# Adaptive layer norm block, 32 sequences: the second norm moved from VectorE to ScalarE, the pooling sum to GpSimd

## The chip, the cores and the metric

The kernel runs on one core of a Trainium2 chip. A core has TensorE (PE in the profile; its weight loads are PEld), VectorE (DVE), ScalarE (ACT), GpSimd (POOL) and the sync engine (SP), which here only issues DMAs. The metric is the device time of one execution in microseconds; smaller is better.

## The reference, cut to what matters

There are 32 sequences (B) of 256 positions (S) of 128 numbers (D). Each goes through a layer norm, an attention block with a local window and a pooled "latent" branch, a gated residual addition, a second layer norm and a small network with weights mixed from eight experts.

```
h = layernorm(x) * (1 + ca) + sa
GK = pool(h @ wgk)                # mean over 4 neighbouring positions: 64 latents
x = x + ga * attention(h)         # local windows of 32, and the 64 latents
h = layernorm(x) * (1 + cb) + sb  # the second norm
x = x + gb * experts(h)           # layernorm(x) = (x - mean) / sqrt(var + 1e-5)
```

## The kernel before, in words

Each engine has its own program, written out by hand; semaphores order them. An engine carries its instructions out in the order in which they stand, and one that waits holds back all that stands behind it.

The first part is a software pipeline over the 32 sequences (`pipeline`, L201). Passage `it` works on up to five sequences, each at another stage: first norm and hT for sequence it (lag 0), projections, scores and maxima for it - 1 (lag 1), exponentials, transposes, values and denominators for it - 2 (lag 2), output projection and residual for it - 3 (lag 3), second norm, h2T and the hidden sum of the gate for it - 4 (lag 4). Passages 0 to 3 are written out, 4 to 31 are a loop, 32 to 35 are written out again. The second part, from about 598 us, applies the mixed expert weights in four groups of eight sequences, and the change does not touch it.

What stands in which order in one passage, as far as the prediction speaks of it:

- VectorE: the maxima and subtractions of the scores (L561, L568), the statistics of both norms (`stats`, L543, giving mv_a and mv_d), then both normalisations (`normed`, L553 to L556, called in L608 for xn_a and in L615 for xn_d), the reciprocal and products of the latent branch (L620 to L629), y_ga (L591), then the reciprocal rden of the local denominators (L639) when TensorE has given them, a_loc (L641), the pooling sum hpT over four positions (L645), the gated products a_gated and rem_g (L652, L654) and the latent maxima (L576), and then the scores of the next sequence.
- GpSimd: the masked keys KM (L347), for each norm ve = var + eps and rstd = ve ** -0.5 (`inv_std`, L335 to L340, on two columns of 128), the two halves of PT_sum (L360), GKBD (L366), the residual addition (L372) and attT (L379).
- ScalarE: copies and exponentials (L413 to L431), then the copies of PL (L438, L441), the four copies of PT out of PSUM (L448), h2T (L452), the ReLU with its sum (L456), hT (L464), the exponentials of the latent branch (L470), tanh (L475).
- TensorE: projections (L851 to L871), the transposes of the latent and local probabilities (L909 to L915, L901), the latent values (L951), which wait for both PL copies, the output projection (L992), the transposes of xn_d (L999), which wait for xn_d, then the values (L932), which wait for all four PT copies, and the denominators (L936), which wait for both halves of PT_sum and release rden. Then r_out (L1006), the gate's first layer (L1016), the transposes of xn_a (L1023), the latent scores (L975) and the scores (L888).

At the start GpSimd also issues DMAs: the scale rows ga to DRAM and, after they have landed, broadcast back as GA (L387, L389), and the expert weights TW (L330, L332). SP issues all other loads, those of the keys KBD (L277) among them, for which the first scores wait.

Of the kernel before, what the change touches and what calls it, by code (L numbers as in the profile page):

```python
# [23 lines left out]
def adaln_block(nc, ins, out):  # L24
# [18 lines left out]
    with ExitStack() as ctx:  # L43
        def sb(name, shape, dt=F32):
            return ctx.enter_context(nc.sbuf_tensor(name, shape, dt))

        def sem(name):
            return ctx.enter_context(nc.semaphore(name))
# [59 lines left out]
        mv_a, mv_d = sb("mv_a", [P, T, 2]), sb("mv_d", [P, T, 2])  # L108
        ve_a, ve_d = sb("ve_a", [P, T]), sb("ve_d", [P, T])
        rstd_a, rstd_d = sb("rstd_a", [P, T]), sb("rstd_d", [P, T])  # L110
        xn_a, xn_d = sb("xn_a", [P, T, D]), sb("xn_d", [P, T, D])
        hT, hpT = sb("hT", [P, S]), sb("hpT", [P, NL])


        QT = [sb(f"QT{k}", [P, S]) for k in range(2)]
# [39 lines left out]
             "ga_ready", "ga_stored", "ga_loaded", "wqT_done", "wqT_ready", "attn_w_ready", "gate_w_done",  # L155
             "gate_w_ready", "masks_ready", "wT_done", "wT_ready"))
        (stat_a, aggr_a, eps_a, rstd_a_s, xn_a_s, xT_done, hT_ready, hp_ready, qk_done, qt_ready, km_ready,
         k_ready, kbd_loaded, pts_ready, gqk_done, gq_ready, gkbd_ready) = (sem(n) for n in (
             "stat_a", "aggr_a", "eps_a", "rstd_a_s", "xn_a_s", "xT_done", "hT_ready", "hp_ready", "qk_done",
             "qt_ready", "km_ready", "k_ready", "kbd_loaded", "pts_ready", "gqk_done", "gq_ready", "gkbd_ready"))  # L160
        (s_ready, mx_ready, s_sub, p_ready, gv_done, gvbd_ready, v_done, vrows_ready, v_stored, vbd_loaded,
         masks_loaded, ls_ready, lmx_ready,
         ls_sub, pl_ready, gates_done, tg_ready) = (sem(n) for n in (
# [149 lines left out]
        def _(pool):  # L313
# [4 lines left out]
                                    pattern=[[-1, P]], channel_multiplier=1).then_inc(mask_ready, 1)  # L318
            nc.gpsimd.memset(minus_half[:], -0.5).then_inc(mask_ready, 1)
            nc.gpsimd.memset(eps_row[:], 1e-5).then_inc(mask_ready, 1)  # L320
            nc.gpsimd.memset(r_out[:], 0.0).then_inc(zeros_ready, 1)
            nc.gpsimd.memset(tri[:], 1.0).then_inc(mask_ready, 1)
            nc.gpsimd.memset(KBD[:], 0.0).then_inc(zeros_ready, 1)
            pool.wait_ge(mask_ready, 5)
            nc.gpsimd.affine_select(out=tri[:], in_=tri[:], compare_op=ALU.is_ge, fill=0.0, base=0,
                                    pattern=[[-1, P]], channel_multiplier=1).then_inc(mask_ready, 1)
            nc.gpsimd.memset(VBD[:], 0.0).then_inc(pv_done, 1)
# [14 lines left out]
            def step(it):  # L342
                if has(it, 1):

                    b = it - 1
                    pool.wait_ge(k_ready, b + 1)
                    nc.gpsimd.tensor_tensor(KM[:], bc(K_ch[:], [P, 4, S], 1), bc(bd_scale[:], [P, 4, S], 2), ALU.mult  # L347
                                            ).then_inc(km_ready, 1)
                if has(it, 0):
                    inv_std(it, aggr_a, mv_a, ve_a, eps_a, rstd_a, rstd_a_s)  # L350
                if has(it, 4):
                    inv_std(it - 4, aggr_d, mv_d, ve_d, eps_d, rstd_d, rstd_d_s)
                if has(it, 2):

                    b = it - 2
                    both = PT[:, 0:G * 2 * S].rearrange("p (g k s) -> p g k s", g=G, k=2)
                    for t in range(T):
                        pool.wait_ge(pt_copied, 4 * b + 2 * (t + 1))
                        tile = slice(t * P, (t + 1) * P)
                        nc.gpsimd.tensor_tensor(PT_sum[:, :, tile], both[:, :, 0, tile], both[:, :, 1, tile], ALU.add  # L360
                                                ).then_inc(pts_ready, 1)
                if has(it, 1):

                    b = it - 1
                    pool.wait_ge(gq_ready, 2 * (b + 1))
                    nc.gpsimd.tensor_tensor(GKBD[0:NL], bc(GKT[:], [NL, LH, NL], 1),  # L366
                                            bc(head[0:NL, 0:LH], [NL, LH, NL], 2), ALU.mult).then_inc(gkbd_ready, 1)
                if has(it, 3):
                    b = it - 3
                    pool.wait_ge(yga_ready, b + 1)  # L370
                    xb = x_all[:, bass.ds(b * S, S)]
                    nc.gpsimd.tensor_tensor(xb, xb, y_ga[:], ALU.add).then_inc(x1_ready, 1)  # L372
                if has(it, 2):
                    b = it - 2

                    pool.wait_ge(ag_ready, b + 1)
                    pool.wait_ge(remg_ready, b + 1)
                    at_least(pool, y_done, b)
                    nc.gpsimd.tensor_tensor(attT[:], a_gated[:], rem_g[:], ALU.add).then_inc(att_ready, 1)  # L379

            def after(it):
                if it == 0:
# [14 lines left out]
        def _(act):  # L397
# [9 lines left out]
            def step(it):  # L407
# [21 lines left out]
                    nc.scalar.copy(V_rows[:].rearrange("p t n -> p (t n)"), WB[3][:, 0:T * D]).then_inc(vrows_ready, 1)  # L429
                if has(it, 2):  # L430
                    probs(it - 2, 3)  # L431
                if has(it, 2):
                    b = it - 2
                    if isinstance(it, int) and it == 2:
                        act.wait_ge(ga_stored, 16)

                    act.wait_ge(lpt_done, 2 * b + 1)
                    nc.scalar.copy(PL[:, :, 0:S].rearrange("p g (t s) -> p t g s", t=T),  # L438
                                   WB[0][:].rearrange("p (t g s) -> p t g s", t=T, g=LG)).then_inc(lpt_copied, 1)
                    act.wait_ge(lpt_done, 2 * b + 2)  # L440
                    nc.scalar.copy(PL[:, :, S:S + P],  # L441
                                   WB[1][:, 0:2 * P].rearrange("p (g s) -> p g s", g=LG)).then_inc(lpt_copied, 1)
                    for q in range(4):

                        act.wait_ge(pt_done, 4 * b + (q + 1))
                        t, gp = divmod(q, 2)
                        dst = PT[:, gp * 4 * S:(gp + 1) * 4 * S].rearrange("p (k s) -> p k s", s=S)[:, :, t * P:(t + 1) * P]
                        nc.scalar.copy(dst, SB[q][:].rearrange("p (k s) -> p k s", s=P)).then_inc(pt_copied, 1)  # L448
# [62 lines left out]
        def _(dve):  # L511
# [83 lines left out]
            def step(it):  # L595
# [9 lines left out]
                if has(it, 0):  # L605
# [2 lines left out]
                    normed(x_all[:, bass.ds(it * S, S)], mv_a, rstd_a, xn_a, xn_a_s)  # L608
                    if isinstance(it, int) and it == 0:
                        modulation()  # L610
                if has(it, 4):
                    b = it - 4
                    dve.wait_ge(rstd_d_s, b + 1)
                    at_least(dve, x2T_done, b)
                    normed(x_all[:, bass.ds(b * S, S)], mv_d, rstd_d, xn_d, xn_d_s)  # L615
                if has(it, 2):

                    b = it - 2
# [16 lines left out]
                if has(it, 2):  # L635
# [3 lines left out]
                    nc.vector.reciprocal(rden[:], SB[2][:, S:2 * S]).then_inc(rden_ready, 1)  # L639
                    dve.wait_ge(rden_ready, b + 1)  # L640
                    nc.vector.tensor_tensor(a_loc[:], SB[2][:, 0:S], rden[:], ALU.mult).then_inc(a_ready, 1)  # L641
                if has(it, 0):

                    dve.wait_ge(hT_ready, it + 1)
                    nc.vector.tensor_reduce(hpT[:], hT[:].rearrange("p (n k) -> p n k", k=POOL), AX.X, ALU.add  # L645
                                            ).then_inc(hp_ready, 1)
                if has(it, 2):
                    b = it - 2
                    dve.wait_ge(a_ready, b + 1)
# [52 lines left out]
            def after(it):  # L702
# [6 lines left out]
                if it == 0:  # L709
# [12 lines left out]
                        then(nc.vector.tensor_scalar(size[:], size[:], 0.25, None, ALU.max))  # L722
                        then(nc.vector.scalar_tensor_tensor(dst[:], sign[:], -1.0, size[:], ALU.add, ALU.mult))
                    nc.vector.memset(wait_carrier[:], 0.0).then_inc(ga_ready, 1)
                    dve.wait_ge(mask_ready, 6)
                    then(nc.vector.tensor_copy(ones_bd[:].rearrange("p (h d) -> p h d", h=4), bc(quad[:], [P, 4, HD], 2)))
                    then(nc.vector.tensor_scalar(pool_bd[:], ones_bd[:], 1.0 / POOL, None, ALU.mult))

# [414 lines left out]
```

## Time and profile before

| what | us |
|---|---|
| median of 2 runs | 773.5 (773.03 and 773.96) |
| span of the profiled execution | 772.4 |
| one passage of the loop, rden to rden | 16.26 |
| PE busy | 701.8 |
| DVE busy | 582.3 |
| ACT busy | 371.3 |
| POOL busy | 292.9 |

The profile is one execution. Its span runs from the first to the last instruction; the median stands 1.1 us above it, and I take that for what lies around the span in the profiled execution too, whose own time is then about 773.5. In a timeline row the first number is the start in us from the span's start, the second the time from the first start to the last end of the merged instructions. Busy shares are averages; what bounds the kernel is read from the chain of waits and from the timelines of one passage.

### The profile page before, as it was taken

The numbers are of one execution on the slowest core, as the hardware profiler recorded it, in microseconds if no ns is written. First come the engines' busy times: TensorE is split into PE (matmuls) and PEld (weight loads), VectorE is DVE, ScalarE is ACT, GpSimd is POOL, SyncE is SP. The second block draws the span as 40 slices with busy tenths as digits, with TensorE's granted clock in tenths as the row PEclk, the third lists the DMA queues.
The fourth block names the chain that finished last, engine by engine and source line by source line (L and its number), as shares of the span: only waits on it lengthen the run. The fifth ranks groups of instructions, "written<-read, shape, count | busy, mean of one in ns | idle before, by whom it ended". The sixth has DMA issues, their size and how long they took to land.

```text
span 772.4 us, 21515 instructions
## 1 busy us (share of the span) xinstructions
PE 701.8 (91%) x7542; PEld 505.3 (65%) x7542; DVE 582.3 (75%) x1313; ACT 371.3 (48%) x878; POOL 292.9 (38%) x351
## 2 busy tenths in 40 slices
PE   5239989999999999999999999999977999999998
PEld 3016656655666656666566666566647989898996
DVE  5326879999989999999999899998885537264542
ACT  2015646555665556655566655566541342433133
POOL 4205635544556445555445564455541000000000
PEclk9569999999999999999999999999996999999999
DMA  3764933222222222232222322222250010000101
GB/s 89 206 73 77 122 57 78 52 60 48 48 65 64 54 54 48 54 75 51 58 48 48 72 57 55 54 48 53 65 62 1 1 35 20 27 27 14 28 20 48
DMA packets 85316, 42.79 MB, mean 55 GB/s; under 512 B 40552, under 2 KB 83880, under 8 KB 85168
## 3 DMA queue, kind: packets, MB, share of 16 engines
q1 hardware_dynamic: 83840, 36.21, 20.7%
q0 software_dynamic: 1456, 6.31, 5.2%
q8 instruction: 13, 0.21, 0.1%
q14 instruction: 7, 0.06, 0.0%
HBM read 16.13 MB, written 8.40 MB: 32 GB/s over the span
## 4 chain that ended last, share of the span: by engine, by line
PE 52%; DVE 22%; issue 10%; POOL 8%; DMA 3%; ACT 2%; SPq 1%; DVEq 1%; POOLq 0%; ACTq 0%
DVE mx L561 10%; PE SB L888 8%; PE SB L836 7%; PE WB L824 7%; DVE xn_d L555 5%; PE WB L975 5%; PE SB L932 4%; PE WB L811 4%; PE SB L811 4%; POOL rstd_d L340 2%; PE WB L1006 2%; POOL rstd_a L340 2%; DMA KBD<-KM 2%; PE SB L936 2%; PE SB L1016 2%
## 5 line engine op out<-in xcount | busy, mean ns | idle before, releaser
L888 PE MATMUL SB<-KBD,QT 128*32 128x512 f32 x1024 | 118.2, 603 | 22.6 <-DMA KBD<-KM 21.6
L347 POOL TENSOR_TENSOR KM<-K_ch,bd_scale 128x1024 f32<-128x1024 f32 x32 | 60.6, 1894 | 142.9 <-ACT K_ch L413 142.9
L561 DVE TENSOR_REDUCE mx<-SB 128x8 f32<-128x512 f32 x128 | 86.7, 678 | 22.9 <-PE SB L888 22.9
L888 PEld LDWEIGHTS SB<-KBD,QT 128*32 128x32 f32 x1024 | 30.6, 111 | 106.3 <-issue 106.3
L506 ACT ACTIVATE Pr<-WB,mb1T 128x256 f32<-128x256 f32 x128 | 49.9, 478 | 75.3 <-PE WB L824 75.3
L360 POOL TENSOR_TENSOR PT_sum<-PT 128x512 f32<-128x512 f32 x64 | 82.1, 1302 | 10.3 <-ACT PT L448 10.3
L568 DVE TENSOR_TENSOR Pr<-SB,mx 128x512 f32<-128x512 f32 x128 | 84.1, 677 | 0.0
L405 ACT ACTIVATE Pr<-Pr 128x512 f32<-128x512 f32 x128 | 80.9, 632 | 5.0 <-DVE Pr L568 1.7
L639 DVE RECIPROCAL rden<-SB 128x256 f32<-128x256 f32 x32 | 56.2, 1757 | 18.9 <-PE SB L936 18.9
L448 ACT COPY PT<-SB 128x512 f32<-128x512 f32 x128 | 65.1, 597 | 0.0
L901 PE MATMUL SB<-ident,Pr 128*128 128x128 f32 x512 | 61.8, 273 | 1.4 <-ACT Pr L405 1.4
L836 PE MATMUL SB<-Pr,GA 128*128 128x256 f32 x256 | 61.0, 381 | 0.0
L824 PE MATMUL WB<-h2T,KBD 128*128 (+1 forms) x256 | 60.2, 380 | 0.0
L901 PEld LDWEIGHTS SB<-ident,Pr 128*128 128x128 f32 x512 | 56.8, 141 | 2.3 <-ACT Pr L405 2.3
L379 POOL TENSOR_TENSOR attT<-a_gated,rem_g 128x256 f32<-128x256 f32 x32 | 23.5, 733 | 89.9 <-DVE a_gated L652 86.8
L555 DVE TENSOR_SCALAR xn_d<-x_all,mv_d,rstd_d 128x128 f32 (+1 forms) x64 | 45.4, 751 | 13.5 <-POOL rstd_d L340 13.5
L824 PEld LDWEIGHTS WB<-h2T,KBD 128*128 128x128 f32 x256 | 48.2, 190 | 6.4
L470 ACT ACTIVATE PlA<-PlA 128x256 f32<-128x256 f32 x32 | 13.3, 417 | 79.4 <-DVE PlA L582 79.4
L836 PEld LDWEIGHTS SB<-Pr,GA 128*128 128x128 f32 x256 | 46.1, 190 | 5.9 <-DVE GA L680 1.0
L975 PE MATMUL WB<-GKBD,GQT 128*128 128x512 f32 (+1 forms) x128 | 47.9, 498 | 0.0
L456 ACT ACTIVATE SB<-SB,gate_b 128x256 f32<-128x256 f32 x32 | 14.3, 448 | 67.3 <-PE SB L1016 67.3
L470 ACT ACTIVATE PlB<-PlB 128x512 f32<-128x512 f32 x32 | 20.1, 630 | 47.5 <-DVE PlB L582 47.5
(190 smaller groups left out, 1484.0 us busy)
## 6 DMA issues: line engine op xcount, KB each, us to landing
KBD<-KM SPq DMA_DIRECT2D x128, 128.0 KB, 2.4
x_all<-in_L_attn_x SPq DMA_DIRECT2D x32, 128.0 KB, 2.1
v_rows<-V_rows SPq DMA_DIRECT2D x32, 128.0 KB, 1.8
TW<-in_L_ffn_TW POOLq DMA_DIRECT2D x16, 256.0 KB, 8.7
VBD<-v_rows SPq DMA_DIRECT2D x128, 32.0 KB, 1.9
GA<-ga_rows POOLq DMA_DIRECT2D x1, 2048.0 KB, 9.9
out_x<-attT SPq DMA_DIRECT2D x16, 128.0 KB, 1.8
out_x<-y_ga SPq DMA_DIRECT2D x16, 128.0 KB, 1.8
```

The source lines that it names most:

```text
L360: nc.gpsimd.tensor_tensor(PT_sum[:, :, tile], both[:, :, 0, tile], both[:, :, 1, tile], ALU.add).then_inc(pts_ready, 1)
L405: nc.scalar.activation(Pr[:, k, :], Pr[:, k, :], ACT.Exp).then_inc(p_ready, 1)
L448: nc.scalar.copy(dst, SB[q][:].rearrange("p (k s) -> p k s", s=P)).then_inc(pt_copied, 1)
L555: nc.vector.tensor_scalar(xn[:, t, :], src[:, t * D:(t + 1) * D], mv[:, t, 0:1], rstd[:, t:t + 1], ALU.subtract, ALU.mult).then_inc(xn_s, 1)
L561: nc.vector.tensor_reduce(mx[:, k, :], SB[k][:].rearrange("p (h j) -> p h j", h=8), AX.X, ALU.max).then_inc(mx_ready, 1)
L568: nc.vector.tensor_tensor(Pr[:, k, :].rearrange("p (w h c) -> p h w c", w=2, h=8), SB[k][:].rearrange("p (h w c) -> p h w c", w=2, h=8), b ...
L811: last = mm((WB if m < 8 else SB)[m % 4][:, k * P:(k + 1) * P], lhsT, Gd[:, bass.ds(g * (J * GB), J * GB)], start=True, stop=True)
L824: last = mm(WB[2 * (j % 2) + c // 2][:, (c % 2) * S:(c % 2 + 1) * S], mW1[:, j, c * P:(c + 1) * P], h2T[:, bass.ds((g * GB + j) * S, S)], ...
L836: last = mm(SB[j % 2][:, 0:S], mW2[:, c, j, :], u[j % 2][:, c, :], start=(c == 0), stop=(c == FC - 1))
L888: last = mm(SB[k][W * q:W * q + W, :].rearrange("p (h j) -> p h j", h=8), QT[hh][:, W * blk:W * blk + W], KBD[:, 8 * hh:8 * hh + 8, W * bl ...
L901: last = nc.tensor.transpose(SB[q][:, k * P:(k + 1) * P], Pr[:, q, o:o + P], ident[:])
L975: mm(WB[1 - t][:, 0:8 * m].rearrange("p (h j) -> p h j", h=8), GQT[:, t * P:(t + 1) * P], GKBD[:, :, 0:m], start=True, stop=True).then_inc ...
```

## The change

The pooling sum over four positions leaves VectorE. GpSimd does it as two additions, 256 to 128 columns and 128 to 64, at the end of its passage, where it waits for hT. The normalisation of the second norm leaves VectorE too. GpSimd computes after rstd_d the negated mean (neg_d) and, after waiting for it, shift_d = -mean * rstd; ScalarE computes xn_d as Identity(x * rstd_d + shift_d), two activations of 128x128, before its PL copies. A buffer of -1 is set up at the start.

```diff
+            nc.gpsimd.memset(minus_one[:], -1.0).then_inc(mask_ready, 1)
...
                 if has(it, 4):
+                    at_least(pool, xn_d_s, T * (it - 4))
                     inv_std(it - 4, aggr_d, mv_d, ve_d, eps_d, rstd_d, rstd_d_s)
+                    nc.gpsimd.tensor_tensor(neg_d[:], mv_d[:, :, 0], minus_one[:], ALU.mult).then_inc(neg_d_s, 1)
+                    pool.wait_ge(rstd_d_s, it - 4 + 1)
+                    pool.wait_ge(neg_d_s, it - 4 + 1)
+                    nc.gpsimd.tensor_tensor(shift_d[:], neg_d[:], rstd_d[:], ALU.mult).then_inc(shift_d_s, 1)
...
+                if has(it, 0):
+
+                    pool.wait_ge(hT_ready, it + 1)
+                    nc.gpsimd.tensor_tensor(hp2[:], hT[:].rearrange("p (m k) -> p m k", k=2)[:, :, 0],
+                                            hT[:].rearrange("p (m k) -> p m k", k=2)[:, :, 1], ALU.add).then_inc(hp2_s, 1)
+                    pool.wait_ge(hp2_s, it + 1)
+                    nc.gpsimd.tensor_tensor(hpT[:], hp2[:].rearrange("p (n k) -> p n k", k=2)[:, :, 0],
+                                            hp2[:].rearrange("p (n k) -> p n k", k=2)[:, :, 1], ALU.add).then_inc(hp_ready, 1)
...
                 if has(it, 2):
                     probs(it - 2, 3)
+                if has(it, 4):
+                    b = it - 4
+                    act.wait_ge(shift_d_s, b + 1)
+                    at_least(act, x2T_done, b)
+                    for t in range(T):
+                        nc.scalar.activation(xn_d[:, t, :], x_all[:, bass.ds(b * S + t * D, D)], ACT.Identity,
+                                             scale=rstd_d[:, t:t + 1], bias=shift_d[:, t:t + 1]).then_inc(xn_d_s, 1)
...
-                if has(it, 4):
-                    b = it - 4
-                    dve.wait_ge(rstd_d_s, b + 1)
-                    at_least(dve, x2T_done, b)
-                    normed(x_all[:, bass.ds(b * S, S)], mv_d, rstd_d, xn_d, xn_d_s)
...
-                if has(it, 0):
-
-                    dve.wait_ge(hT_ready, it + 1)
-                    nc.vector.tensor_reduce(hpT[:], hT[:].rearrange("p (n k) -> p n k", k=POOL), AX.X, ALU.add
-                                            ).then_inc(hp_ready, 1)
```

The order on ScalarE in the loop, from the last exponential to h2T, before. ISA and REGISTER_ALU rows compute addresses and semaphore values; they are no work on data.

```order
L405 ACTIVATE Pr<-Pr 128x512 [waits s_sub]
L437 ISA
L438 COPY PL<-WB 128x2x2x128 [waits lpt_done]
L440 REGISTER_ALU
L441 COPY PL<-WB 128x2x128 [waits lpt_done]
L445 REGISTER_ALU
L448 COPY PT<-SB 128x4x128 [waits pt_done] x4
L451 REGISTER_ALU
L452 ISA [waits x2T_done]
```

And in the changed kernel:

```order
L420 ACTIVATE Pr<-Pr 128x512 [waits s_sub]
L449 REGISTER_ALU
L190 REGISTER_ALU [waits shift_d_s]
L452 ISA [waits x2T_done]
L452 ACTIVATE xn_d<-x_all,shift_d,rstd_d 128x128
L452 ISA
L452 ACTIVATE xn_d<-x_all,shift_d,rstd_d 128x128
L459 ISA
L460 COPY PL<-WB 128x2x2x128 [waits lpt_done]
L462 REGISTER_ALU
L463 COPY PL<-WB 128x2x128 [waits lpt_done]
L467 REGISTER_ALU
```

The two activations that write xn_d, and the wait for shift_d ahead of them, now stand ahead of the PL and PT copies, which stand unchanged behind them.

The order on GpSimd in the loop, from rstd_a to PT_sum, before:

```order
L340 TENSOR_TENSOR rstd_a<-ve_a,minus_half 128x2 [waits eps_a]
L337 ISA
L338 TENSOR_TENSOR ve_d<-mv_d,eps_row 128x2 [waits aggr_d]
L340 TENSOR_TENSOR rstd_d<-ve_d,minus_half 128x2 [waits eps_d]
L358 ISA
L360 TENSOR_TENSOR PT_sum<-PT 128x4x128 [waits pt_copied]
L358 REGISTER_ALU
L360 TENSOR_TENSOR PT_sum<-PT 128x4x128 [waits pt_copied]
```

And in the changed kernel, where the last row's wait, pt_copied, is for ScalarE's PT copies:

```order
L342 TENSOR_TENSOR rstd_a<-ve_a,minus_half 128x2 [waits eps_a]
L190 ISA
L339 ISA [waits xn_d_s]
L340 TENSOR_TENSOR ve_d<-mv_d,eps_row 128x2 [waits aggr_d]
L342 TENSOR_TENSOR rstd_d<-ve_d,minus_half 128x2 [waits eps_d]
L356 TENSOR_TENSOR neg_d<-mv_d,minus_one 128x2
L359 TENSOR_TENSOR shift_d<-neg_d,rstd_d 128x2 [waits neg_d_s,rstd_d_s]
L365 ISA
L367 TENSOR_TENSOR PT_sum<-PT 128x4x128 [waits pt_copied]
```

Two more instructions, neg_d and shift_d, stand between rstd_d and PT_sum.

The order on GpSimd at the start, from the first norm of passage 1 to the broadcast of GA, before:

```order
L338 TENSOR_TENSOR ve_a<-mv_a,eps_row 128x2 [waits aggr_a]
L340 TENSOR_TENSOR rstd_a<-ve_a,minus_half 128x2 [waits eps_a]
L366 TENSOR_TENSOR GKBD<-GKT,head 64x512 [waits gq_ready]
L387 DMA ga_rows<-PT 32x128 [waits ga_ready]
L389 DMA GA<-ga_rows 128x4096 [waits ga_stored]
```

And in the changed kernel, where hp is the buffer hp2:

```order
L340 TENSOR_TENSOR ve_a<-mv_a,eps_row 128x2 [waits aggr_a]
L342 TENSOR_TENSOR rstd_a<-ve_a,minus_half 128x2 [waits eps_a]
L373 TENSOR_TENSOR GKBD<-GKT,head 64x512 [waits gq_ready]
L390 TENSOR_TENSOR hp<-hT 128x128 [waits hT_ready]
L393 TENSOR_TENSOR hpT<-hp 128x64 [waits hp2_s]
L402 DMA ga_rows<-PT 32x128 [waits ga_ready]
L404 DMA GA<-ga_rows 128x4096 [waits ga_stored]
```

The two additions, which wait for hT of passage 1, now stand ahead of the DMAs of ga, GA and the expert weights.

## Rows read from the trace of the kernel before

**Rows 1.** The page, the chain that ended last, shares by engine.

```profile
PE 52%; DVE 22%; issue 10%; POOL 8%; DMA 3%; ACT 2%; SPq 1%; DVEq 1%; POOLq 0%; ACTq 0%
```

**Rows 2.** The chain of waits around 345 us: start, us, what.

```profile
345.36 1.30 DVE xn_d L555
...
346.71 0.44 PE SB L999 x2
```

**Rows 3.** Timeline of VectorE, one passage: start, us, instruction, [idle before].

```profile
332.52 1.76 DVE L639 RECIPROCAL rden<-SB 128x256 f32<-128x256 f32 x1 [0.34 <-PE SB L936]
...
334.67 0.42 DVE L645 TENSOR_REDUCE hpT<-hT 128x64 f32<-128x256 f32 x1
335.01 0.42 DVE L652 SCALAR_TENSOR_TENSOR a_gated<-tg,a_loc 128x256 f32<-128x256 f32 x1
...
344.16 0.60 DVE L555 TENSOR_SCALAR xn_a<-x_all,mv_a,rstd_a 128x128 f32 x2 [0.34 <-POOL rstd_a L340]
345.10 1.55 DVE L555 TENSOR_SCALAR xn_d<-x_all,mv_d,rstd_d 128x128 f32 x2 [0.33 <-POOL rstd_d L340]
...
348.78 1.76 DVE L639 RECIPROCAL rden<-SB 128x256 f32<-128x256 f32 x1 [0.32 <-PE SB L936]
```

**Rows 4.** Timeline of ScalarE, the same passage.

```profile
343.36 0.57 ACT L438 COPY PL<-WB 128x512 f32<-128x512 f32 x1
343.82 0.37 ACT L441 COPY PL<-WB 128x256 f32<-128x256 f32 x1
...
347.41 0.57 ACT L452 ACTIVATE h2T<-SB,sbT,cb1T 128x256 f32 x1 [1.29 <-PE SB L999]
```

**Rows 5.** Timeline of GpSimd, the same passage.

```profile
344.09 0.20 POOL L338 TENSOR_TENSOR ve_d<-mv_d,eps_row 128x2 f32<-128x2 f32 x1
344.37 0.69 POOL L340 TENSOR_TENSOR rstd_d<-ve_d,minus_half 128x2 f32<-128x2 f32 x1
```

**Rows 6.** Timeline of TensorE, the same passage.

```profile
342.47 1.91 PE L901 MATMUL SB<-ident,Pr 128*128 128x128 f32 x16
344.31 0.42 PE L951 MATMUL WB<-PL,GVBD 128*32 128x128 f32 x8
...
348.64 0.71 PE L1006 MATMUL WB<-rem_n,r_out 128*128 128x128 f32 x4
```

**Rows 7.** Timeline of all engines, first passage after the loop.

```profile
555.07 0.57 ACT L438 COPY PL<-WB 128x512 f32<-128x512 f32 x1
...
556.95 2.53 POOL L360 TENSOR_TENSOR PT_sum<-PT 128x512 f32<-128x512 f32 x2 [1.11 <-ACT PT L448]
...
559.53 0.64 PE L936 MATMUL SB<-PT_sum,ones_bd 128*32 128x256 f32 x8 [0.34 <-POOL PT_sum L360]
...
560.24 1.76 DVE L639 RECIPROCAL rden<-SB 128x256 f32<-128x256 f32 x1 [1.28 <-PE SB L936]
...
562.49 0.42 DVE L652 SCALAR_TENSOR_TENSOR a_gated<-tg,a_loc 128x256 f32<-128x256 f32 x1
```

**Rows 8.** ScalarE groups by form: line, op, shapes, count | busy us, mean ns | idle.

```profile
L452 ACT ACTIVATE h2T<-SB,sbT,cb1T 128x256 f32 x28 | 15.9, 567 | 35.3 <-PE SB L999 35.3
...
L429 ACT COPY V_rows<-WB 128x256 f32<-128x256 f32 x32 | 11.4, 357 | 0.7 <-PE WB L863 0.7
...
L494 ACT COPY gate_w1T<-WB 128x128 f32<-128x128 f32 x1 | 0.3, 266 | 0.6 <-PE WB L1083 0.6
```

**Rows 9.** Timeline of TensorE, the loop's first passage.

```profile
101.71 1.44 PE L932 MATMUL SB<-PT,VBD 128*32 128x64 f32 x48 [2.84 <-issue]
...
103.99 1.08 PE L1006 MATMUL WB<-rem_n,r_out 128*128 128x128 f32 x4
```

**Rows 10.** Busy time by stretch: us, PE, PEld, DVE, ACT, POOL, PEclk, DMA, GB/s.

```profile
101.00:105.00 4.00, 3.29 (x62) 2.48 (x63) 0.90 (x1) 0.00 (x0) 0.44 (x1) 0.57 0.11 23
```

**Rows 11.** Timeline of the start, GpSimd and TensorE.

```profile
24.74 0.72 POOL L387 DMA_DIRECT2D ga_rows<-PT  x1
...
50.00 5.39 PE L888 MATMUL SB<-KBD,QT 128*32 128x512 f32 x32 [21.57 <-DMA KBD<-KM]
```

More of the change, by code:

```diff
@@ L110, in adaln_block @@
         rstd_a, rstd_d = sb("rstd_a", [P, T]), sb("rstd_d", [P, T])
+        minus_one, neg_d, shift_d = sb("minus_one", [P, T]), sb("neg_d", [P, T]), sb("shift_d", [P, T])
         xn_a, xn_d = sb("xn_a", [P, T, D]), sb("xn_d", [P, T, D])
-        hT, hpT = sb("hT", [P, S]), sb("hpT", [P, NL])
+        hT, hp2, hpT = sb("hT", [P, S]), sb("hp2", [P, S // 2]), sb("hpT", [P, NL])
         QT = [sb(f"QT{k}", [P, S]) for k in range(2)]
@@ L157, in adaln_block @@
         (stat_a, aggr_a, eps_a, rstd_a_s, xn_a_s, xT_done, hT_ready, hp_ready, qk_done, qt_ready, km_ready,
-         k_ready, kbd_loaded, pts_ready, gqk_done, gq_ready, gkbd_ready) = (sem(n) for n in (
+         k_ready, neg_d_s, shift_d_s, hp2_s, kbd_loaded, pts_ready, gqk_done, gq_ready, gkbd_ready) = (sem(n) for n in (
              "stat_a", "aggr_a", "eps_a", "rstd_a_s", "xn_a_s", "xT_done", "hT_ready", "hp_ready", "qk_done",
-             "qt_ready", "km_ready", "k_ready", "kbd_loaded", "pts_ready", "gqk_done", "gq_ready", "gkbd_ready"))
+             "qt_ready", "km_ready", "k_ready", "neg_d_s", "shift_d_s", "hp2_s", "kbd_loaded", "pts_ready", "gqk_done", "gq_ready", "gkbd_ready"))
         (s_ready, mx_ready, s_sub, p_ready, gv_done, gvbd_ready, v_done, vrows_ready, v_stored, vbd_loaded,
@@ L323, in _ @@
             nc.gpsimd.memset(KBD[:], 0.0).then_inc(zeros_ready, 1)
-            pool.wait_ge(mask_ready, 5)
+            pool.wait_ge(mask_ready, 6)
             nc.gpsimd.affine_select(out=tri[:], in_=tri[:], compare_op=ALU.is_ge, fill=0.0, base=0,
@@ L724, in after @@
                     nc.vector.memset(wait_carrier[:], 0.0).then_inc(ga_ready, 1)
-                    dve.wait_ge(mask_ready, 6)
+                    dve.wait_ge(mask_ready, 7)
                     then(nc.vector.tensor_copy(ones_bd[:].rearrange("p (h d) -> p h d", h=4), bc(quad[:], [P, 4, HD], 2)))
```

## The prediction

> **What bounds the kernel now.** I read the shares of the chain first, then the chain around one passage of the loop, then the timelines of the engines in that passage, at last the passages that have no partner in the loop.
>
> The chain lies on TensorE for 52%, on VectorE for 22% and on GpSimd for 8% [rows 1]: no single engine sets the end, a ring through several does. In the passage from 332.52 to 348.78 it runs from VectorE to rstd_d on GpSimd (344.37 for 0.69) [rows 5], from there to xn_d on VectorE, and from there to TensorE's transposes at 346.71 [rows 2]. Behind these stand the values and denominators, which release rden, and with rden VectorE begins anew: rden to rden is 348.78 - 332.52 = 16.26 us [rows 3]. So xn_d is on the path. Its two instructions take 1.55 us where the same two for xn_a take 0.60 [rows 3], since the second runs into GpSimd's PT_sum.
>
> There is a second way through the passage, and it decides here. ScalarE starts the PL copies at 343.36 [rows 4], 1.7 us before rstd_d is ready (344.37 + 0.69 = 345.06) [rows 5], and the PT copies follow them, then PT_sum, the denominators, rden. In passage 32, which has no first norm, this way is what arrives last: PL copy 555.07, PT_sum 556.95, denominators 559.53 after a wait of 0.34 us for PT_sum, rden 560.24 [rows 7]. From PL to rden it is 5.17 us; in the loop 348.78 - 343.36 = 5.42 [rows 3, 4]. So the second way is only 0.25 us shorter than the one through xn_d. Whatever delays the PL copies by more than 0.25 us delays the passage.
>
> **The change part by part.**
>
> **The pooling sum** leaves VectorE. The row is 0.42 us, but without it a_gated begins 562.49 - 560.24 = 2.25 us after rden instead of 335.01 - 332.52 = 2.49 [rows 3, 7]: a gain of 0.24 us, because the wait for a_loc is then bare. VectorE works without a break from rden to the statistics, so all of it counts, and rstd_d ends at 345.06 - 0.24 = 344.82. On GpSimd the two additions stand behind attT. TensorE reads hpT only in its next projections, behind all the scores, and GpSimd waits for ScalarE meanwhile, so I put them at nothing (bounds 0 and +1 a passage, if the stride of two made them several times slower).
>
> **neg_d and shift_d.** Two operations on two columns. The nearest row is ve_d, 0.20 us, with the next starting 0.28 after it; the other is rstd_d, a power, 0.69 [rows 5]. I take the first, a product being nearer to a sum: neg_d starts at the end of rstd_d less some 0.04 of overlap, shift_d 0.28 later, and ends 0.20 after that, at 344.82 - 0.04 + 0.28 + 0.20 = 345.26. Bound from above: 0.69 each, +1.0. Behind them waits PT_sum, but that will be later anyway.
>
> **xn_d on ScalarE.** ScalarE's order puts it ahead of PL. This is the heart of it: PL and PT need nothing from the second norm and now wait for it. ScalarE's start behind a wait with an address computed after it: the transposes end at 346.71 + 0.44 = 347.15, h2T starts at 347.41, so 0.26 [rows 2, 4]; VectorE needed 0.04 (345.06 to 345.10) [rows 3, 5], which is the lower bound. I take 0.27: start 345.53. One Identity with scale and bias from columns takes 0.567 for 256 columns; copies of 256 and 128 columns differ by 0.357 - 0.266 = 0.091 [rows 8], so 0.476 each. Each starts 0.11 before the one ahead of it ends, as the two PL copies do (343.36 + 0.57 against 343.82) [rows 4], and an address stands between them, 0.05: together 0.476 + 0.476 - 0.11 + 0.05 = 0.89. Bounds: 0.27 + 0.17, as for plain copies, and 0.567 whole, twice. The PL copy may start 0.11 before their end, at 345.53 + 0.89 - 0.11 = 346.31. That is 2.95 us later than 343.36. Then the 5.17 of the second way: rden at 351.48, a passage of 351.48 - 332.52 = 18.96, which is 2.7 us more than 16.26. The bounds taken together give +2.0 and +3.9.
>
> The xn_d that VectorE loses gives nothing back: its 1.55 us were worth 0.25, up to where the second way takes over, and that way is now 3 us late.
>
> **TensorE.** Its transposes of probabilities end at 342.47 + 1.91 = 344.38, or 344.14 with the gain above; the latent values start 0.95 us after the PL copy (343.36, 344.31) [rows 4, 6], so at 347.26. Today there is no gap there; the changed kernel has one of 3.1 us in each passage. What such a gap does, one place shows: in the loop's first passage TensorE stood idle 2.84 us before 101.71 [rows 9], and in 101 to 105 its mean granted clock was 0.57, so it had fallen from 2.4 to 1.2 GHz and came back [rows 10]. The work lost is (1 - 0.57) x 4 = 1.7 us; 0.34 of it would lie in TensorE's wait for PT_sum [rows 7], so a fall costs at most 1.4 on the path. The r_out group took 1.08 instead of 0.71 us [rows 6, 9], which says that part of it lies behind rden, where TensorE is ahead. I take 1.0 (bounds 0 and 1.4), and 8 passages in 10, because one gap with one fall doesn't say that each has it.
>
> The Trainium skill (TensorE: Matmul & The Clock Gate, HAM oscillation) describes a kernel whose TensorE waits in each tile, is set back to half clock each time and pays each time. By that rule every passage falls: 27 x 1.4 = 38 us instead of the 21 that I enter. The row of the loop's first passage agrees with the rule, for one gap.
>
> **Outside the loop.** 27 passages of the loop are alike (4 to 31 without the first). The first has the idle 2.84 us already, and I let ScalarE's wait fall into it: 0 (bounds -2 and +3). In passages 32 and 33, where the statistics come earlier, the same reckoning gives +1.9 and +2.5, and in 34 and 35 the longer way to xn_d +0.3: 4.7.
>
> **The start.** The first scores wait 21.57 us for the keys, which land at 50.00, while GA and the expert weights are being moved [rows 11]. The changed kernel has the two additions ahead of those DMAs: the one at 24.74 starts 1 to 2 us later, while VectorE, which no longer waits for hT, makes the masks about 1 us sooner. So the keys get ahead of part of the other traffic. I take -4 (bounds -15, where it all falls away, and +1).
>
> **The sum.** 27 x 2.7 = 73; + 0 + 4.7 - 4 = 74; the clock 27 x 0.8 x 1.0 = 21; in all +95. The profiled execution's own time is its span 772.4 and about 1.1 around it, 773.5, which is the median of the runs shown. 773.5 + 95 = 868.5; I say 868.
>
> **The rivals.**
>
> Clock stays up: the gap of 3.1 us is followed by dense work and TensorE keeps its 2.4 GHz. For it: in the loop's other passages there is hardly an idle time, so the trace has one case only. Against it: that case. 773.5 + 74 = 847.
>
> Faster: ScalarE's wait is harmless, because shift_d would come before the PL copies, and what counts is that the collision of xn_d with PT_sum is gone. The place is the PL copy at 343.36; it decides from the moment when shift_d is ready before it, and it comes at 345.26 by the sum. If it held, the loop would run at the second way's 16.26 - 0.25 - 0.24 = 15.8, 27 x 0.49 = 13 less, and with the start -4: 756. For it: 1.55 against 0.60 us on the path [rows 3]; against it: 1.9 us that cannot go.
>
> The start gives back much more: keys and GA no longer meet, -15 instead of -4: 857. For it: the DMA order; against it: the expert weights follow on the same queues at once.
>
> GpSimd as the bound: the strided additions take several us and TensorE waits for hpT. The price is +1 or more a passage, 895. GpSimd is idle for most of that time, so I give it little.
>
> **How the numbers follow.** Forecast 0.68, clock up 0.17, large gain at the start 0.08, slow additions 0.04, faster 0.02, and 0.01 that the change comes out within 2%, which is about what a measurement of this kernel can tell from no change. Range: from 840 (clock up, and the cheap end of ScalarE's start) to 888 (a fall in each passage at 1.4, which is 885, and a little for GpSimd). Faster 0.02, same 0.01, slower 0.97.
>
> **What would show it.** Right: a passage of 19 to 20.5 us; ScalarE idle about 2 us before xn_d, released by GpSimd's shift_d; the PL copy 3 us later within the passage; TensorE idle some 3 us before the latent values, released by ScalarE, and a granted clock of 0.5 in many short stretches; rden waiting for the denominators and these for PT_sum; the keys landing a few us before 50. Wrong: a passage below 17, PL copies that don't move, a granted clock of 1.00 through the loop (then 847), or TensorE waiting for GpSimd's hpT.

## The result: 858.2 us, 11% slower, and where the time went

The changed kernel takes 858.2 us (median of 2 runs, 856.89 and 859.43) against 773.5, a ratio of 1.108 with a 95% interval from 1.106 to 1.111. Forecast were 868 us and a range from 840 to 888. The profiled execution took 856.89 us, its span is 855.2: 82.8 more than the 772.4 of before.

The page's busy times and the shares of the chain by engine, for the changed kernel (the chain answers to [rows 1]):

```profile
PE 722.6 (85%) x7542; PEld 528.4 (62%) x7542; DVE 530.2 (62%) x1217; ACT 401.2 (47%) x942; POOL 323.4 (38%) x480
...
PE 37%; DVE 27%; issue 17%; POOL 8%; ACT 5%; DMA 2%; DVEq 1%; SPq 1%; ACTq 0%; POOLq 0%
```

VectorE lost 52 us of work (582.3 to 530.2) and the kernel became 85 us longer. ScalarE, which was hardly on the chain, has 5% of it now, and "issue", time in which the profile shows nothing that is waited for, grew from 10% to 17%. TensorE has the same 7542 matmuls and is busy 21 us longer: a sign that it ran part of them at a lower clock.

One passage without a fall of the clock, from rden at 368.96 to rden at 387.93, 18.97 us. GpSimd in it (answers to [rows 5]; start, us, instruction):

```profile
380.59 0.69 POOL L342 TENSOR_TENSOR rstd_d<-ve_d,minus_half 128x2 f32<-128x2 f32 x1
381.24 0.19 POOL L356 TENSOR_TENSOR neg_d<-mv_d,minus_one 128x2 f32<-128x2 f32 x1
381.58 0.20 POOL L359 TENSOR_TENSOR shift_d<-neg_d,rstd_d 128x2 f32<-128x2 f32 x1
384.65 2.52 POOL L367 TENSOR_TENSOR PT_sum<-PT 128x512 f32<-128x512 f32 x2 [2.87 <-ACT PT L470]
```

ScalarE in the same passage (answers to [rows 4]):

```profile
381.98 0.88 ACT L452 ACTIVATE xn_d<-x_all,shift_d,rstd_d 128x128 f32 x2 [2.27 <-POOL shift_d L359]
382.76 0.56 ACT L460 COPY PL<-WB 128x512 f32<-128x512 f32 x1
383.23 0.37 ACT L463 COPY PL<-WB 128x256 f32<-128x256 f32 x1
383.49 2.05 ACT L470 COPY PT<-SB 128x512 f32<-128x512 f32 x4
```

TensorE (answers to [rows 6], and its L948 to the denominators of [rows 7]):

```profile
383.64 0.42 PE L963 MATMUL WB<-PL,GVBD 128*32 128x128 f32 x8 [2.95 <-ACT PL L463]
...
385.31 0.38 PE L1011 MATMUL SB<-ident,xn_d 128*128 128x128 f32 x2
385.67 1.21 PE L944 MATMUL SB<-PT,VBD 128*32 128x64 f32 x64
387.22 0.64 PE L948 MATMUL SB<-PT_sum,ones_bd 128*32 128x256 f32 x8 [0.34 <-POOL PT_sum L367]
387.79 0.71 PE L1018 MATMUL WB<-rem_n,r_out 128*128 128x128 f32 x4
```

VectorE at its end (answers to [rows 3]):

```profile
387.93 1.76 DVE L656 RECIPROCAL rden<-SB 128x256 f32<-128x256 f32 x1 [1.25 <-PE SB L948]
```

Read from top to bottom this is one ring: ScalarE, done with its exponentials, stands idle for 2.27 us until GpSimd has shift_d; then come xn_d, the PL copies, the PT copies, the two halves of PT_sum, the denominators, rden. The latent values on TensorE wait 2.95 us, for PL copies that before were made while the statistics were still being worked out. The transposes of xn_d, for which the second norm is needed at all, don't wait any more.

The waits between 120 and 600 us, in total, times, longest, show that it is so in every passage, once each:

```profile
PE WB L963 <- ACT PL L463: 73.4, 25, 3.0
...
POOL PT_sum L367 <- ACT PT L470: 69.0, 24, 2.9
...
ACT xn_d L452 <- POOL shift_d L359: 56.4, 25, 2.3
```

The next passage, from 387.93 to 407.83, has the same work and takes 19.90. Busy time by stretch (us; PE, PEld, DVE, ACT, POOL with counts; granted clock; share and GB/s of DMA): first the passage without a fall, then this one nearly whole, then four stretches inside it.

```profile
368.96:387.93 18.97, 15.69 (x201) 10.39 (x202) 13.30 (x33) 10.67 (x25) 8.76 (x14) 1.00 0.23 48
387.93:407.80 19.87, 16.94 (x201) 11.56 (x201) 13.31 (x32) 10.68 (x25) 10.48 (x16) 0.91 0.22 46
...
399.50:402.50 3.00, 0.18 (x2) 0.00 (x0) 0.45 (x2) 1.56 (x5) 1.04 (x3) 1.00 0.86 176
402.50:404.00 1.50, 1.39 (x30) 1.25 (x32) 0.00 (x0) 1.50 (x5) 0.39 (x1) 0.51 0.04 8
404.00:406.00 2.00, 2.00 (x24) 1.83 (x20) 1.28 (x3) 0.51 (x2) 2.00 (x2) 0.52 0.00 0
406.00:407.83 1.83, 1.83 (x75) 1.30 (x74) 0.50 (x3) 0.56 (x1) 1.79 (x3) 1.00 0.00 0
```

TensorE is all but idle from 399.5 to 402.5 (0.18 us of work), then is granted 1.2 GHz instead of 2.4 for about 3.5 us, and has its full clock back before rden. Its rows there:

```profile
402.61 0.66 PE L963 MATMUL WB<-PL,GVBD 128*32 128x128 f32 x8 [2.93 <-ACT PL L463]
...
404.66 1.22 PE L1004 MATMUL WB<-w_out_half,attT 128*128 128x128 f32 x4
...
407.14 0.62 PE L948 MATMUL SB<-PT_sum,ones_bd 128*32 128x256 f32 x8
407.69 0.71 PE L1018 MATMUL WB<-rem_n,r_out 128*128 128x128 f32 x4
```

From the latent values to the denominators it takes 407.14 - 402.61 = 4.53 us, against 387.22 - 383.64 = 3.58 without a fall. The 0.34 us of waiting for PT_sum are gone, so the work grew by 1.29 and the path by 0.95; over the whole passage it is 0.93. Of the loop's 27 like passages 20 have such a fall, three in a row and then one without, and on the mean a fall costs 0.87.

The balance of the two spans, from the starts of rden in either trace:

| stretch | before | after | difference |
|---|---|---|---|
| to the first rden | 68.11 | 58.39 | -9.7 |
| the next two passages, the loop's first among them | 35.99 | 35.47 | -0.5 |
| 27 like passages of the loop | 440.11 | 529.57 | +89.5 |
| passages 32 and 33 | 31.43 | 36.74 | +5.3 |
| behind the last rden of the local branch | 196.8 | 195.0 | -1.7 |
| sum | | | +82.8 |

(Differences are taken before rounding.) The +89.5 are 27 times 2.67 for the ring (18.97 against a mean of 16.30) and 20 times 0.87 for the clock: 72.1 and 17.4.

The -9.7 at the start. The issue of the keys' DMAs, of GA's, and the first scores, in the changed kernel ([rows 11] are those of before):

```profile
28.07 2.54 SPq L278 DMA_DIRECT2D KBD<-KM  x4
...
30.12 0.59 POOL L404 DMA_DIRECT2D GA<-ga_rows  x1 [3.17 <-DMA ga_rows<-PT]
...
40.02 5.65 PE L900 MATMUL SB<-KBD,QT 128*32 128x512 f32 x32 [12.74 <-DMA KBD<-KM]
```

In the kernel before, the same two issues stood almost together:

```profile
29.78 2.69 SPq L277 DMA_DIRECT2D KBD<-KM  x4
...
29.97 0.59 POOL L389 DMA_DIRECT2D GA<-ga_rows  x1 [4.50 <-DMA ga_rows<-PT]
```

A lead of the keys of 0.19 us has become one of 2.05, and the scores start 10 us sooner. Experiments 5, 6 and 8 below are about this.

### The profile page after: what moved, and what is told of

The parts are those of the page before. It is cut to its first block, busy times and chain, and to the rows that moved or that the text cites. A ratio compares the mean times of both kernels' runs of the same rounds, so it can differ in the third digit from the quotient of the medians.

```text
span 855.2 us, 21704 instructions
## 1 busy us (share of the span) xinstructions
PE 722.6 (85%) x7542; PEld 528.4 (62%) x7542; DVE 530.2 (62%) x1217; ACT 401.2 (47%) x942; POOL 323.4 (38%) x480
## 4 chain that ended last, share of the span: by engine, by line
PE 37%; DVE 27%; issue 17%; POOL 8%; ACT 5%; DMA 2%; DVEq 1%; SPq 1%; ACTq 0%; POOLq 0%
DVE mx L583 9%; PE SB L848 7%; PE WB L836 7%; DVE rden L656 6%; PE SB L944 4%; PE WB L963 4%; PE WB L823 4%; PE SB L823 3%; PE WB L1004 3%; POOL PT_sum L367 3%; POOL rstd_d L342 3%; PE SB L948 2%; ACT xn_d L452 2%; DVE a_loc L658 2%; DVE st_a L568 2%
## 5 line engine op out<-in xcount | busy, mean ns | idle before, releaser
L900 PE MATMUL SB<-KBD,QT 128*32 128x512 f32 x1024 | 118.5, 604 | 14.4 <-DMA KBD<-KM 12.7
L367 POOL TENSOR_TENSOR PT_sum<-PT 128x512 f32<-128x512 f32 x64 | 80.2, 1274 | 88.9 <-ACT PT L470 88.9
L637 DVE RECIPROCAL rlden<-WB 128x128 f32<-128x128 f32 x32 | 30.6, 958 | 126.4 <-PE WB L963 126.4
L963 PE MATMUL WB<-PL,GVBD 128*32 128x128 f32 x384 | 23.9, 312 | 86.2 <-ACT PL L463 86.2
L583 DVE TENSOR_REDUCE mx<-SB 128x8 f32<-128x512 f32 x128 | 86.7, 677 | 14.7 <-PE SB L900 14.7
L963 PEld LDWEIGHTS WB<-PL,GVBD 128*32 128x32 f32 x384 | 13.4, 118 | 93.6 <-ACT PL L463 93.4
L452 ACT ACTIVATE xn_d<-x_all,shift_d,rstd_d 128x128 f32 (+1 forms) x64 | 28.1, 485 | 72.3 <-POOL shift_d L359 72.3
```

Of the source, the lines that this page charges most:

```text
L583: nc.vector.tensor_reduce(mx[:, k, :], SB[k][:].rearrange("p (h j) -> p h j", h=8), AX.X, ALU.max).then_inc(mx_ready, 1)
L900: last = mm(SB[k][W * q:W * q + W, :].rearrange("p (h j) -> p h j", h=8), QT[hh][:, W * blk:W * blk + W], KBD[:, 8 * hh:8 * hh + 8, W * bl ...
L963: last = mm(WB[0][q:q + W, den * P:(den + 1) * P], ones_bd[:] if den else GVBD[:, k, g, :], PL[:, g, (t + k) * P:(t + k + 1) * P], start=( ...
```

## The experiments

My theory: ScalarE's wait for shift_d, placed ahead of the PL copies, sets the passage, and falls of TensorE's clock in the gap add to it; the pooling sum gains a little by itself. Its rivals: the activations themselves or GpSimd's added work are what costs, wherever they stand; and the lower clock has another cause than the gap. For the start, the theory is that the gain is the keys' lead over GA's transfer; the rival, that it comes from the masks being made sooner.

**1. The normalisation alone.** The changed kernel with the pooling sum back on VectorE:

```diff
-                    pool.wait_ge(hT_ready, it + 1)
...
                     nc.vector.tensor_tensor(a_loc[:], SB[2][:, 0:S], rden[:], ALU.mult).then_inc(a_ready, 1)
+                if has(it, 0):
+
+                    dve.wait_ge(hT_ready, it + 1)
+                    nc.vector.tensor_reduce(hpT[:], hT[:].rearrange("p (n k) -> p n k", k=POOL), AX.X, ALU.add
+                                            ).then_inc(hp_ready, 1)
```

> The second norm's move alone: GpSimd computes shift_d, ScalarE computes xn_d ahead of the PL copies; the pooling sum stays on VectorE. My theory (the whole slowdown comes from ScalarE waiting for shift_d ahead of the PL and PT copies, and from the clock falls behind it): a passage without a fall 18.97 + 0.24 = 19.2 us, falls in about three of four passages, and the keys land at 50 again instead of 40, so about 858 + 6.5 + 10 = 875. Rival (GpSimd's two additions for the pooling are a part of the slowdown): faster than the changed kernel, below 858.

Measured: 876.8 us, ratio 1.133 (1.131 to 1.135). A passage without a fall takes 19.22 us, 0.25 more than with both parts; the gap on TensorE is 3.05 us and about five passages in six have a fall. So the normalisation is the whole loss and more, and the pooling sum is worth 0.25 a passage here too.

**2. The pooling sum alone.** The kernel before with the two additions on GpSimd in place of VectorE's sum.

> The pooling sum's move alone: two additions on GpSimd; the second norm stays on VectorE. My theory: VectorE's stretch is 0.24 us shorter in each passage, 16.30 becomes 16.05, and the keys land about 10 us earlier at the start, so 773.5 - 6.6 - 10 = 757. Rival (TensorE waits for GpSimd's hpT, or the additions delay GpSimd's other work): a passage above 16.3 and 773 or more.

Measured: 757.2 us, ratio 0.979 (0.977 to 0.980). The 27 passages take 433.4 us, 6.7 fewer than before, and the first scores start at 41.02 instead of 50.00. At the first rden 8.0 us of the start's gain are there (60.16 against 68.11); with the passages' 6.7 that is 14.7 of the 16.0 measured, and the rest lies in passages 32 and 33 (0.3) and behind them. The two halves of the change add up nearly: +103.6 and -16.0 make +87.7, measured are +84.7.

**3. The same activations, behind the PT copies.** The changed kernel; the block of xn_d on ScalarE is moved, not altered.

```diff
                 if has(it, 2):
                     probs(it - 2, 3)
-                if has(it, 4):
-                    b = it - 4
-                    act.wait_ge(shift_d_s, b + 1)
...
+                if has(it, 4):
+                    b = it - 4
+                    act.wait_ge(shift_d_s, b + 1)
...
                 if has(it, 4):
                     b = it - 4
                     act.wait_ge(x2T_done, b + 1)
```

> The changed kernel with ScalarE's xn_d block moved behind the four PT copies, ahead of h2T; all else as in the changed kernel. My theory (the place in ScalarE's order is the cause, not the work): the PL copies start 0.24 us earlier in the passage than before, xn_d ends at about the same moment as it did on VectorE, a passage of about 16.4 us, no clock falls in the loop, and with the start's gain of 10 about 766. Rival (the work itself, GpSimd's two more operations and ScalarE's slower xn_d, is the cause): a passage above 18, 815 or more.

Measured: 764.6 us, ratio 0.990 (0.987 to 0.993): 94 us fewer than the changed kernel, by the place of two instructions. ScalarE and TensorE in one passage:

```profile
300.98 0.57 ACT L453 COPY PL<-WB 128x512 f32<-128x512 f32 x1
...
301.71 2.04 ACT L463 COPY PT<-SB 128x512 f32<-128x512 f32 x4
303.61 0.90 ACT L469 ACTIVATE xn_d<-x_all,shift_d,rstd_d 128x128 f32 x2
...
304.57 0.44 PE L1011 MATMUL SB<-ident,xn_d 128*128 128x128 f32 x2 [0.73 <-ACT xn_d L469]
```

The activations take 0.90 us as before and have no idle time ahead of them; the passage is 16.32 us and the 27 like passages have no fall. So neither the activations nor GpSimd's work are the cost; the wait in front of PL is. It also shows that the move gains nothing even here: 16.32 against 16.03 with xn_d on VectorE (experiment 2), because xn_d is now ready only after the PT copies, at 304.51, and TensorE waits 0.73 us for it.

**4 and 9. Filling the gap on TensorE.** The changed kernel; in the gap TensorE makes ten (then eighteen) transposes of the identity into a free half of a PSUM bank, which nobody reads. The ring stays as it is.

```diff
+                if has(it, 4):
+                    for k in range(10):
+                        nc.tensor.transpose(WB[3][:, 2 * P + (k % 2) * P:3 * P + (k % 2) * P], ident[:], ident[:])
                 pe.wait_ge(lpt_copied, 2 * (b + 1))
```

> The changed kernel with ten transposes of the identity on TensorE, into columns of WB3 that nothing reads then, ahead of the wait for the PL copies, so that its idle time of 2.95 us in a passage becomes some 0.6. The waits stay. If the falls of the granted clock make three of four passages 0.8 to 0.9 us longer, they go: all passages 18.97 us, granted clock 1.00 through the loop, 858 - 18 = 840. Rival (the longer passages have another cause and the falls are only seen beside them): still 19.8 in three of four and 858; or the ten transposes themselves delay the latent values, then above 858.

> As e4_fill with 18 transposes instead of ten: e4's ten took 1.26 us and left 1.85 us of idle time in a passage, behind which the clock still fell in 6 of 27 passages; 18 take 2.3 and leave 0.8. Clock theory: no fall left in the loop, all 27 passages 18.97, granted clock 1.00 there, about 843.5 - 6 = 838. Rival (some falls have another cause than the idle time): falls stay, 843.

Measured: 843.5 us with ten (ratio 1.091, 1.089 to 1.093) and 840.6 with eighteen (1.086, 1.084 to 1.089). Ten of them take only 1.26 us where I had expected about 2.3, so that 1.85 us of the gap stayed; eighteen leave 0.97. The stretches of the loop, first the changed kernel, then ten, then eighteen (the last one only up to 600 us; over all its 27 like passages, 512.03 us, the clock is 1.00 too); columns as above, the granted clock is the third number from the end:

```profile
93.86:623.43 529.57, 447.91 (x5401) 303.41 (x5402) 359.24 (x865) 288.28 (x675) 258.37 (x379) 0.94 0.22 47
```

```profile
93.30:610.14 516.84, 460.35 (x5671) 315.21 (x5672) 359.22 (x864) 288.07 (x675) 259.31 (x380) 0.98 0.22 48
```

```profile
93.30:600.00 506.70, 472.84 (x5796) 330.44 (x5788) 357.71 (x860) 283.86 (x666) 255.71 (x376) 1.00 0.22 48
```

Passages with a fall: 20, 6 and none of 27. TensorE does more work in each of these and the kernel gets shorter, by 17.6 us from the changed kernel to the one with eighteen; the 27 passages alone give 17.5 (529.57 against 512.03), which is the 17.4 of the balance. With the clock up all passages take 18.96: the ring by itself. So the lower clock comes from the gap.

The falls over all runs, by the idle time ahead of the latent values: 3.05 us, five in six (experiment 1); 2.95, 20 of 27; 1.85, 6 of 27; 0.97, none. The Trainium skill (TensorE: Matmul & The Clock Gate, HAM oscillation) has TensorE set back in each tile of a kernel that waits some 3 to 5 us for a DMA in each. The gap here is a little shorter, 2.95 us, and the clock fell in three passages of four, and in fewer with a shorter gap; that every passage falls, as the prediction worked out from that rule, did not come.

**5 and 6. The start: GA's DMAs held back.** The kernel before; GpSimd waits ahead of the ga, GA and TW DMAs, for the second hT (experiment 5) or until the first keys have landed (6).

```diff
                     pool.wait_ge(ga_ready, 1)
+                    pool.wait_ge(hT_ready, 2)
```

In experiment 6 the added line is another:

```diff
+                    pool.wait_ge(kbd_loaded, 64)
```

> The kernel before, but GpSimd waits for hT of passage 1 ahead of the DMAs of ga, GA and the expert weights (the place where the changed kernel's additions hold them back); VectorE's masks are not earlier. Theory A (the start's gain of 10 us comes from the weights' DMAs standing later): keys at about 40 us, 764. Theory B (it comes from the masks and with them the keys' own DMAs being issued 1.7 us sooner, and GA's DMA, which waits for the landing of ga, moves by only 0.2): keys within 2 us of 50, 773.

> The kernel before, but GpSimd issues the DMAs of ga, GA and the expert weights only when the first keys have landed. Both theories of the start: with no GA and expert traffic beside them the four key DMAs of 128 KB need a few us each and the keys are there at about 34 instead of 50, unless TensorE then waits for the values' blocks or for GA: between 757 and 765. If the keys' time is set by something else than that traffic (the masks' own packets): still about 48 and 772.

Measured: 766.2 us (ratio 0.990, 0.988 to 0.992) and 763.3 (0.987, 0.985 to 0.989). The scores start at 43.25 and at 34.10. In experiment 5 GA's issue moved by 1.33 us (29.97 to 31.30), and the keys' not at all; that alone is worth 6.75 us at the scores. In experiment 6 much of the 15.9 us is gone again soon: at the first rden 10.9 are left (57.24 against 68.11), mostly since TensorE stands still for 4.02 us in the middle of the values of that passage, on nothing that the profile names ("issue"), and the next three passages take 1.5 us more together than before. Whether GA's later transfer is behind either was not looked into.

**8. The start: the additions behind the DMAs.** Experiment 2, but in passage 1 GpSimd issues its DMAs first and adds afterwards, so that only VectorE's half of the effect is left.

```diff
-                if has(it, 0):
+                if has(it, 0) and not (isinstance(it, int) and it == 1):
                     pooled(it)
...
+                if it == 1:
+                    pooled(1)
```

> As e2_pool_only, but in passage 1 GpSimd's two additions stand behind the DMAs of ga, GA and the expert weights, so that the masks are 1 us earlier and the DMAs are too. Theory A (the DMAs' place): the gain is gone, keys at 48 to 50, about 766. Theory B (keys issued sooner, relative to GA): if GA's DMA goes out at 29 or before, the keys have lost their lead, 46 to 49; if it stays at 30, they keep it, 40 to 41 and 757.

Measured: 765.9 us (ratio 0.989, 0.987 to 0.991); the scores start at 51.64, later than before and than either theory had it, though the keys' DMAs are issued at 28.62 instead of 29.78. So masks and keys that are sooner by themselves give nothing. One line over all of them, from one profile each. The keys go out in four DMAs, 0.6 us apart; "landing" is the time from the issue of each to its landing:

| kernel | keys issued | GA issued | lead of the keys | landing of the four | first scores |
|---|---|---|---|---|---|
| before | 29.78 | 29.97 | 0.19 | 9.6, 13.6, 17.5, 18.2 | 50.00 |
| 8 | 28.62 | 28.97 | 0.35 | 2.5, 13.5, 17.1, 21.0 | 51.64 |
| 1 | 29.12 | 29.49 | 0.37 | 2.6, 14.4, 18.1, 22.3 | 53.41 |
| 5 | 29.72 | 31.30 | 1.58 | 2.4, 2.5, 2.5, 11.5 | 43.25 |
| 2 | 28.60 | 30.35 | 1.75 | 2.4, 2.5, 2.5, 10.4 | 41.02 |
| after | 28.07 | 30.12 | 2.05 | 2.4, 2.6, 2.5, 9.9 | 40.02 |
| 6 | 29.65 | 37.23 | 7.58 | 2.5, 2.5, 2.4, 2.4 | 34.10 |

(The profiled execution of experiment 1 took 5.5 us more than its median; its start belongs to that execution.) On the median a key DMA of 128 KB takes 15.6 us to land before and 2.5 after; first the kernel before, then the changed one, in the first 60 us:

```profile
KBD<-KM SPq DMA_DIRECT2D x4, 128.0 KB, 15.6
```

```profile
KBD<-KM SPq DMA_DIRECT2D x8, 128.0 KB, 2.5
```

(The second row has eight issues, since the keys of the next sequence fall into the 60 us as well; the median of the first four alone is 2.5 too, and it hides the fourth, at 9.9, for which the scores wait.) The transfers share the 16 DMA engines, which before are 90% busy or more from 24 to 49.5 us. So it goes by steps: a key DMA issued 0.3 us or more ahead of GA's 2 MB has landed after 2.4 to 2.6 us, one issued 0.2 us ahead of it or later takes 9.6 to 22.3. With three of the four ahead the scores start at 40 to 43 us, with one or none at 50 to 53. The Trainium skill (DMA: Bandwidth & Descriptors, Queues, rings and completion order) says that a DMA engine takes the queues that have work for it in turn, a packet at a time. That fits, but no run here shows single packets taking turns.

**7. A next step: TensorE's transposes inside the values.** Experiment 2; the transposes of xn_d, for which TensorE waits, are moved behind the values and ahead of the denominators.

> The pooling sum on GpSimd, the norm on VectorE (as in e2_pool_only), and TensorE's transposes of xn_d between the values and the denominators, where it waits for PT_sum anyway, instead of ahead of the values. Theory: then xn_d is off the path and the second way (PL, PT, PT_sum, denominators) alone sets the passage: 5.17 + 10.84 - 0.24 = 15.77 against 16.03, so 757.2 - 27 x 0.26 = 750. Rival: VectorE is full (xn_d, rlden, rem_n, GVBD, y_ga stand ahead of rden) and nothing is won: 757.

Measured: 756.3 us, ratio 0.977 (0.976 to 0.979), a passage of 15.94 against 16.03. Both expectations missed: the passage shrank by 0.09 us, not by 0.26, and what holds it is neither the old wait nor VectorE. The chain in this window has, but for short "issue" pieces, TensorE rows alone (L943 values, L926 transposes of xn_d, L949 denominators, L1015 r_out, L892 scores):

```profile
301.40 1.19 PE SB L943 x63
302.59 0.37 PE SB L926 x2
302.96 0.63 PE SB L949 x8
303.59 0.10 issue
303.69 0.68 PE WB L1015 x4
...
306.32 3.57 PE SB L892 x32
```

Here TensorE is busy 15.87 of 16.00 us (301 to 317), at a granted clock of 1.00, and is the bound. Nothing that only shortens VectorE's part can help from here.

**10. The two gains together.** Experiment 7 with GA's DMAs behind the landed keys, as in 6.

> The best of both parts: pooling sum on GpSimd, second norm on VectorE, TensorE's transposes of xn_d between values and denominators (e7_t_in_values), and the DMAs of ga, GA and the expert weights only behind the landing of the first keys (e6_dma_last). If the two gains add: keys at 33 to 34 instead of 40 to 41, some of it given back in passages 1 to 3, 756.3 - 4 = 752. Rival: the later GA and weights delay y_ga or starve TensorE's instructions by as much, 756 to 758.

Measured: 752.1 us (749.5 to 753.8), ratio 0.972 (0.969 to 0.975): the scores start at 32.98, passages settle at 15.95. This version beats both kernels. It has the pooling half of the change without the other, and two changes of order.

## Why the prediction was right

The forecast was slower, 868 us, and the mechanism is the one it named: shift_d late, PL copies behind it, TensorE's gap, falls of the clock. By its steps:

- **The pooling sum, 0.24 us gained a passage, GpSimd's additions free.** Right. It is 0.25 in experiment 2 as well as between experiment 1 and the changed kernel. The additions take 0.40 and 0.29 us and end at 373.57; TensorE takes hpT up at 376.51.
- **neg_d and shift_d at 0.20 each.** Right: 0.19 and 0.20. shift_d begins 0.34 after neg_d instead of 0.28, since it waits for neg_d to have ended.
- **xn_d on ScalarE, 0.89 us for the two after a start of 0.27.** 0.88 and 0.20 (381.78 to 381.98). The mean of one was taken as 476 ns and is 485. The Trainium skill (ScalarE: Activation LUTs, What ACT_TABLE_LOAD costs) would give 186 + 0.833 x 128 + 2 x 93 = 479 ns, an estimate that agrees with the row.
- **The second way of 5.17 us from PL to rden, a passage of 18.96.** 387.93 - 382.76 = 5.17, and 18.97. The small errors above cancel. The base was off: I took one passage, 16.26, where the mean of the 27 is 16.30, and so the step was +2.67 and not +2.7: 72 instead of 73.
- **The PL copy 2.95 us later in the passage, the gap of 3.1 us on TensorE.** 2.96 later (13.80 behind rden instead of 10.84), and a gap of 2.95.
- **The falls, 8 in 10 at 1.0 us.** 20 of 27 at 0.87: 17.4 instead of 21.6 (27 x 0.8 x 1.0, written down as 21). The way of costing held: the granted clock says (1 - 0.515) x 3.5 = 1.7 us lost, as in [rows 10]; 1.29 of it appear between the latent values and the denominators, and the wait for PT_sum swallows 0.34. I had let all but 0.34 through as the bound and taken 1.0. Where the other 0.4 goes was not looked into.
- **Passages 32 and 33, +4.4 together (+1.9, +2.5).** +1.9 and +3.4; the second has a fall of its own, of about 0.85, which I had not entered there. For 34 and 35, and all behind them, I said +0.3; the stretch came out at -1.7. The kernels of experiments 5 and 6, which have the instructions of before in that stretch, took 195.1 and 195.4 there against 196.8, so it is neither of the two moves; what gives the difference stays open.
- **The loop's first passage, 0.** -0.3.
- **The start, -4.** This term was mis-sized: -9.7. I named the cause (the additions delay the DMAs, the masks come sooner, the keys get ahead) and took "part of the other traffic". What failed is to price it by the microseconds moved (DMAs 1 to 2 later, masks 1 sooner): GA's own issue came only 0.15 later, the keys' 1.71 sooner. Experiments 5, 2 and 8 and the changed kernel show what stands in its place: what counts is how many of the four key DMAs go out ahead of GA. Three of them ahead are worth 10 us at the scores, and the fourth, in experiment 6, 6 more.

The rivals: the clock that stays up would have been right without the falls (847; experiment 9, where it does stay up, has 840.6). The large gain at the start was forecast to give 857 and came closest to the number, 858.2, but that is luck: the start gave -9.7 and not -15, and the falls of the clock and the end of the kernel made up for it. Slow additions didn't come, and ScalarE's wait was not harmless. The faster rival's passage of 15.8 us would hardly have been reached in any case: in experiment 7 TensorE's own work holds it at 15.94.

From the +95 of the sum to the +82.8 of the spans: -5.7 at the start, -4.2 for the clock in the loop, -0.8 for the ring's base, +0.9 in passages 32 and 33, -2.0 behind them, -0.5 in the two passages behind the first rden; the rest is rounding.

## What to carry to other kernels

An instruction moved to an idle engine takes its wait along, and everything that stands behind it on that engine then waits too: look for what the new engine does next and who needs it, and put the moved work behind that (here two activations ahead of the PL copies cost 94 us more than behind the PT copies). Before taking work off an engine, read which second way through the ring comes just behind it; here 1.55 us of VectorE's time were worth at most 0.25 by the rows of before, and 0.09 where experiment 7 took the wait for them away. At a start where two transfers compete, look at which pieces are issued first: holding back the one that isn't needed yet brought the first scores 7 and 16 us forward, of which 7 and 10 were left at the end (experiments 5 and 6).

## What the runs showed of the hardware that was not expected

- The falls of TensorE's clock come in a strict order. With 2.95 us of idle time in each passage three passages fall and the fourth doesn't, over the whole loop, with periods of 18.97, 19.90, 19.85 and 19.79. The passage of 18.97 had a gap of 2.95 us and no fall, the next one a gap of 2.93 and a fall, so the gap in front of it doesn't settle it alone.
- Ten transposes of 128x128 of the identity took 1.26 us, 0.13 each. That is the rate of the transposes of probabilities in [rows 6] (1.91 us for 16, 0.12 each) and half of what experiment 4 had been planned with.
- The first scores move by 7 to 10 us when the keys' lead over GA grows by less than 2 us, because two or three more of the four key DMAs land after 2.5 us instead of 10 to 18 (table of experiment 8).
